# A five-layer graph network on one core: the first unit behind each batch norm rectified in two parts, and high pieces four units behind the rectifiers

## What is computed

```python
def _gin_conv(x, src, dst, edge_attr, w1, b1, bn_w, bn_b, w2, b2, ew, eb):
    edge_emb = edge_attr @ ew.T + eb
    n = x.shape[0]
    agg_x = jax.ops.segment_sum(x[src], dst, num_segments=n) + x
    agg_e = jax.ops.segment_sum(edge_emb, dst, num_segments=n) + eb
    h = jnp.concatenate([agg_x, agg_e], axis=1)
    h = h @ w1.T + b1                                  # to 256 features
    mean = jnp.mean(h, axis=0)
    var = jnp.mean((h - mean) ** 2, axis=0)
    h = (h - mean) * jax.lax.rsqrt(var + BN_EPS) * bn_w + bn_b
    h = jax.nn.relu(h)
    return h @ w2.T + b2                               # back to 128
...
h = jnp.maximum(_layernorm(x, axis=-1), 0.0)
for l in range(5):
    h = _gin_conv(h, ...)
    if l < 4:
        h = jax.nn.relu(h)
return x + h
```

## Time and profile before

| what | us |
|---|---|
| median of 3 runs | 654.82 (654.66 to 655.7) |
| the profiled execution, its own time | 658.63 |
| its span, first to last instruction | 656.8 |
| PE busy | 613.7 (93%) |
| VectorE busy | 331.2 (50%) |
| ScalarE busy | 261.0 (40%) |

### The profile page before, as it was taken

The page is one execution under the profiler, slowest core; times in us unless marked ns, Lnnn a source line. Parts: engine busy times, 40 slices in busy tenths (PEclk is TensorE's granted clock), DMA queues, the critical chain, the costliest instruction groups (busy, mean ns, idle before and its releaser), DMA issues.

```text
span 656.8 us, 12887 instructions
## 1 busy us (share of the span) xinstructions
PE 613.7 (93%) x5447; PEld 373.6 (57%) x5447; DVE 331.2 (50%) x663; ACT 261.0 (40%) x569; POOL 72.4 (11%) x90
## 2 busy tenths in 40 slices
PE   6788898978999989999999999999999999999996
PEld 6676787745555544844446644447544457444456
DVE  6799999979999928522113421125311216101034
ACT  0268977755677715601115411117211128012133
POOL 5550135510221100000000000000000000000000
PEclk9899999998999999999999999999999999999999
DMA  5981001000000000000000100000100000100033
GB/s 143 318 277 11 2 4 27 6 4 5 4 3 4 4 5 1 26 9 1 1 1 1 33 1 1 1 1 1 33 1 1 1 1 2 31 2 1 1 96 102
DMA packets 13320, 19.22 MB, mean 29 GB/s; under 512 B 2263, under 2 KB 7397, under 8 KB 13251
## 3 DMA queue, kind: packets, MB, share of 16 engines
q1 hardware_dynamic: 12099, 16.00, 8.1%
q0 software_dynamic: 1152, 2.20, 1.4%
HBM read 16.26 MB, written 1.60 MB: 27 GB/s over the span
## 4 chain that ended last, share of the span: by engine, by line
PE 59%; DVE 2%; ACT 1%; issue 0%; POOLq 0%; DVEq 0%
PE bank L1338 39%; PE bank L1402 9%; PE bank L1374 8%; PE bank L1368 2%; ACT h L1458 1%; DVE bn_stats L1562 1%; DVE h L1583 0%; DVE h L1584 0%; PE bank L1385 0%; PE bank L252 0%; DVE h L1603 0%; ACT bn_small L1471 0%; PE bank L1327 0%; DVE bn_small L1578 0%; DVE bn_small L1577 0%
## 5 line engine op out<-in xcount | busy, mean ns | idle before, releaser
L1338 PE MATMUL bank<-adj,h_pieces 128*128 128x504 bf16 (+1 forms) x1372 | 263.5, 351 | 0.0
L1338 PEld LDWEIGHTS bank<-adj,h_pieces 128*128 128x128 f16 x1372 | 123.0, 97 | 141.4 <-issue 10.2
L1562 DVE BATCH_NORM_STATS2 bn_stats<-bank 128x6 f32<-128x504 f32 (+1 forms) x70 | 42.8, 627 | 219.3 <-PE bank L1374 218.7
L971 ACT ACTIVATE adj<-bank 128x450 bf16<-128x450 f32 x175 | 95.3, 547 | 65.3 <-PE bank L829 60.0
L1449 ACT ACTIVATE aggT<-bank 128x504 f32<-128x504 f32 x24 | 14.2, 590 | 261.0 <-PE bank L1374 223.7
L444 DVE TENSOR_TENSOR h<-iota_lo,h 128x1536 bf16<-128x1536 bf16 (+2 forms) x95 | 87.5, 921 | 8.2 <-PE bank L829 7.1
L853 PE MATMUL bank<-h,adj 128*17 128x40 f32 (+11 forms) x1752 | 79.3, 206 | 11.2 <-DVE h L639 6.2
L829 PE MATMUL bank<-h 128*128 128x75 bf16 x1064 | 69.3, 201 | 17.5 <-DVE h L444 16.1
L453 PE MATMUL bank<-adj,h_pieces 128*128 128x450 bf16 x343 | 83.6, 356 | 1.6 <-issue 1.6
L829 PEld LDWEIGHTS bank<-h 128*128 128x128 bf16 x1064 | 54.9, 100 | 49.8 <-DVE h L444 30.0
L853 PEld LDWEIGHTS bank<-h,adj 128*17 128x17 f32 x1752 | 69.2, 104 | 18.1 <-DVE h L639 10.5
(11 more groups left out here) (151 smaller groups left out, 364.5 us busy)
## 6 DMA issues: line engine op xcount, KB each, us to landing
adj<-attr SPq DMA_DIRECT2D x1, 2524.5 KB
adj<-attr SPq DMA_DIRECT2D x1, 1963.5 KB
weights<-wpack SPq DMA_DIRECT2D x5, 323.0 KB
out<-h SPq DMA_DIRECT2D x6, 256.0 KB
adj<-attr SPq DMA_DIRECT2D x1, 1402.5 KB
adj<-attr SPq DMA_DIRECT2D x2, 561.0 KB
h<-mpack SPq DMA_DIRECT2D x5, 179.0 KB
adj<-order SPq DMA_DIRECT2D x2, 202.0 KB, 2.9
```

The source lines that it names most:

```text
L971: nc.scalar.activation(out_view(u), bank_view(n % CNT_BANKS), ACT.Copy).then_inc(s_ev, 1)
L1338: last = nc.tensor.matmul(agg_ps[b][:, 0:w], hp[:, k, s, :], adj[:, k, c * LW:c * LW + w], start=(k == 0 and s == 0), stop=stop and s == p ...
L1562: V.bn_stats(stats[:, h, ds(c * 6, 6)], w1_ps[b][h][:, 0:cols]).then_inc(st_last if last and h == 1 else st_done, 1)
```

## The change

The first unit is rectified in two parts, its first tile (128 columns) and its other three (384 columns), on ScalarE (half 0) and on VectorE (half 1). PE's unit 0 waits for the first part before tile 0, and for the second before tile 1. A semaphore is added for ScalarE's first part; VectorE's now counts two steps a layer. And high(u) stands behind the rectifiers of unit u+4 on ScalarE, where it stood behind those of unit u+2.

```diff
--- before.py
+++ after.py
@@ -1247,6 +1247,7 @@
             mv_done = sem("bn_moments_done")
             sd_done = sem("bn_deviation_done")
             relu0_done = sem("first_unit_second_half_done")
+            relu_tile = sem("first_tile_first_half_done")
             bn_c = sem("bn_chain")
             bn_ready = sem("bn_ready")
             relu_done = sem("relu_done")
@@ -1255,8 +1256,9 @@
             hi_done = sem("high_piece_done")
             o_done = sem("out_added")
             o_st = sem("out_stored")
-            BN_STEPS = 4
+            BN_STEPS = 5
             WSTEPS, M_STEPS = 16, 4
+            HI_LAG = 4
 
             def tiles_of(u):
                 return 1 if u == UNITS - 1 else 4
@@ -1389,14 +1391,19 @@
                     def project(l, u, final):
                         if u == 0 and not final:
                             pe.wait_ge(w2_scaled, l + 1)
-                        pe.wait_ge(relu_done, l * UNITS + u + 1)
                         if u == 0:
-                            pe.wait_ge(relu0_done, l + 1)
+                            pe.wait_ge(relu_tile, l + 1)
+                            pe.wait_ge(relu0_done, 2 * l + 1)
+                        else:
+                            pe.wait_ge(relu_done, l * UNITS + u + 1)
                         if u >= 2:
 
                             pe.wait_ge(t_done, l * UNITS + u - 1)
                         r = rows_of(u)
                         for j in range(tiles_of(u)):
+                            if u == 0 and j == 1:
+                                pe.wait_ge(relu_done, l * UNITS + 1)
+                                pe.wait_ge(relu0_done, 2 * l + 2)
                             for h in range(2):
                                 a = u * UW + j * P
                                 last = nc.tensor.matmul(w2_ps[u % 2][0:r, j * P:(j + 1) * P], h1[:, h, a:a + r],
@@ -1461,21 +1468,28 @@
 
                     def relu(l, u):
 
-                        for h in range(1 if u == 0 else 2):
-                            v = h1[:, h, u * UW:min((u + 1) * UW, N_NODES)]
-                            last = nc.scalar.activation(v, v, ACT.Relu, bias=shift[:, h:h + 1], scale=scale[:, h:h + 1])
+                        def part(h, a, b):
+                            v = h1[:, h, a:b]
+                            return nc.scalar.activation(v, v, ACT.Relu, bias=shift[:, h:h + 1], scale=scale[:, h:h + 1])
+                        if u == 0:
+                            part(0, 0, P).then_inc(relu_tile, 1)
+                            last = part(0, P, UW)
+                        else:
+                            for h in range(2):
+                                last = part(h, u * UW, min((u + 1) * UW, N_NODES))
                         last.then_inc(relu_done, 1)
 
                     def normalise(l, final):
                         act.wait_ge(mv_done, l + 1)
                         nc.scalar.activation(sd[:, :], mv[:, :, 1], ACT.Sqrt, bias=cst[:, EPSC:EPSC + 1]).then_inc(sd_done, 1)
                         act.wait_ge(bn_ready, l + 1)
-                        for u in range(UNITS + 2):
+                        for u in range(UNITS + HI_LAG):
                             if u < UNITS:
                                 relu(l, u)
-                            if u >= 2 and not final:
-                                act.wait_ge(t_done, l * UNITS + u - 1)
-                                nc.scalar.activation(hp_view(u - 2, 0), unit_view(0, u - 2), ACT.Relu).then_inc(hi_done, 1)
+                            if u >= HI_LAG and not final:
+                                act.wait_ge(t_done, l * UNITS + u - HI_LAG + 1)
+                                nc.scalar.activation(hp_view(u - HI_LAG, 0), unit_view(0, u - HI_LAG), ACT.Relu
+                                                     ).then_inc(hi_done, 1)
 
                     def layer(l, final):
                         act.wait_ge(l_wp, (l + 1) * 16)
@@ -1577,11 +1591,12 @@
                         steps.then(V.tensor_tensor(ms, mean_b, scale, ALU.mult))
                         V.tensor_tensor(shift, wp[:, BNB:BNB + 2], ms, ALU.subtract).then_inc(bn_ready, 1)
 
-                        v = h1[:, 1, 0:UW]
                         dve.wait_ge(h1_ev, (l + 1) * CHUNKS)
                         dve.wait_ge(bn_ready, l + 1)
-                        steps.then(V.tensor_scalar(v, v, scale[:, 1:2], shift[:, 1:2], ALU.mult, ALU.add))
-                        V.tensor_scalar(v, v, 0.0, None, ALU.max).then_inc(relu0_done, 1)
+                        for a, b in ((0, P), (P, UW)):
+                            v = h1[:, 1, a:b]
+                            steps.then(V.tensor_scalar(v, v, scale[:, 1:2], shift[:, 1:2], ALU.mult, ALU.add))
+                            V.tensor_scalar(v, v, 0.0, None, ALU.max).then_inc(relu0_done, 1)
                         assert steps.n == BN_STEPS
 
                     def add_bias(l, u):
```

## The result

The changed kernel takes 657.56 us in the median of 22 runs, the one before 655.25 in 22 runs beside them. The ratio is 1.0027, 95% interval 1.0018 to 1.0035, so 1.8 us more (1.2 to 2.3). The two means, 657.40 and 655.63, differ by 1.8 as well, the two medians by 2.3. The forecast was +1.9. One execution of the kernel with the split alone, further down, took 1038.12 us at a mean granted clock of 0.557; it is left out of that kernel's ratio.

What follows compares the result with a forecast made beforehand. TensorE was taken as the bound, busy 613.7 of 656.8 us, with the head on its path. Four layers at +0.52 and the last at -0.19 gave +1.9 us on the 654.82 median: 656.8, range 655.2 to 658.0.

Steps and rivals of the forecast that it cites:

- The size and the place of the loss: Projection of the first four layers: TensorE waits at units 4 and 5, last unit starts 0.52 us later a layer.
- The step on the head: Unit 0's split rectifiers: first tile 0.51 us earlier, 0.31 given back, unit 1 0.19 to 0.20 us a layer earlier.
- the wait at unit 4: Projection: bias(2), queued behind low(0) on VectorE, comes late, so TensorE waits 0.56 us before unit 4.
- Low(0) waits: Sign in the changed profile: VectorE's low pieces wait for the high piece, about 1 us at the first.
- the second wait, in front of unit 5: Projection: after high(1) the same steps make TensorE wait another 0.14 us; sign given as 0.1 to 0.2.
- The last layer: No high pieces there, so only the head counts: -0.19 us, the residual's load just in time for unit 2.
- B: Rival: the wait at unit 4 does not bite, faster, -1.0 us (653.9) or -2.6 (652.3); chance 0.08.
- C: Rival: wait half as long, ScalarE's row shorter, loss 0.1 to 0.35 a layer; +0.8 us, 655.6; chance 0.22.
- D: Rival: split at its upper price or TensorE slow to restart behind each wait; +3.6 us, 658.4; chance 0.08.
- E: Rival: holes in the projection lower TensorE's granted clock to 1.2 GHz for two units; 14 us, 669; chance 0.02.

Runs made afterwards that it cites:

- the split alone: The changed kernel with `HI_LAG = 2` (two-part first unit, high pieces two units behind as before); 655.35 us, ratio 0.9995 to the kernel before.
- lag 5: The changed kernel with `HI_LAG = 5`, high pieces five units behind instead of four; 663.13 us against 655.41 for the kernel before, ratio 1.0117.
- the lag alone: The kernel before with high pieces four units behind, unit 0 in one part; 656.07 us against 655.46, ratio 1.0005.
- the change with the moved wait: The changed kernel, last layer's VectorE wait for the residual's load moved from first bias to first residual addition; 656.33 us, ratio 1.0014 to the kernel before.

## Why the prediction was right

**The size and the place of the loss: right.** The working set unit 4's start at R + 8.75 and unit 6's at R + 12.47. Measured are R + 8.73 and, by the bias of unit 5 less 0.27 us (the distance that the working had between the two), 12.44; unit 6's first record itself stands at R + 12.61, before at R + 12.12, the same 0.49. High(0) was put at R + 6.65 and came at 6.64, since ScalarE's spacing of 0.707 and the overlap of its parts held (128 columns took 493 ns for the 478 that I worked out, 384 took 693 for 692). The chain high(0), low(0), bias(2), unit 4 was shown by three doses: lag 4 without the split +0.21 a layer, with it +0.49, lag 5 +1.75; and by the run that takes the bias additions out from behind the low pieces and leaves the rest, -0.06.

**The step on the head: the price of VectorE's part was too low.** I took 256 ns for the multiply-add on 128 columns, from a line through 353 ns at 256 columns (L1514, one pointer) and 547 at 512 (L1583, two pointers). It took 348 ns, and 475 for 384, in the groups of lines by form of the changed kernel:

```profile
L1598 DVE TENSOR_SCALAR h<-h,bn_small 128x384 f32<-128x384 f32 x5 | 2.4, 475 | 0.0
...
L1598 DVE TENSOR_SCALAR h<-h,bn_small 128x128 f32<-128x128 f32 x5 | 1.7, 348 | 0.5
```

The two forms were not of one kind (one pointer and a multiply, against two pointers and a multiply-add). So unit 1 starts 0.06 us earlier, not 0.19. This cost the sum nothing in four layers, for the reason the prediction gave: the end of the projection hangs on ScalarE's row alone, and the head's gain is used up in front of the wait. But the wait at unit 4 was smaller too, where I had 0.56: without it unit 4 starts at R + 8.39, as the trace of the split alone has it, and it started at R + 8.73, 0.34 us later. Starting again cost another 0.07, since the first record behind a hole is 0.18 us ahead of the second where the spacing inside a group is 0.11; I had no term for that. The loss against before is nearly the same (0.49 for 0.52), since it is counted from before's start of unit 4. Two of my signs were off as well. Low(0) waits 1.57 us, and I wrote about 1 us where my own working gives 551.68 - 549.94 = 1.74. And the second wait, in front of unit 5, has 0.07 us where I had 0.14: unit 5's first record is 1.93 us behind unit 4's, 0.14 more than a unit's 1.787, and half of that is the new start.

**The last layer: mis-sized, and the sum came out in part by luck.** I had -0.19, with a margin of 0.02 us at unit 2 for the residual's load. The traced execution has +0.48. In eight traces (before, the change, and six of the runs above that keep the wait at bias(0)) bias(0) starts 7.90 to 8.65 us behind the issue of the load's second part, with the same instructions in front. The forecast took one early landing (7.90, the shortest of all) as the rule. The kernel before can wait for the load until R + 4.05 without loss (unit 2 asks at R + 4.88, and starts 0.83 behind bias(0) at the earliest); in its own trace the load was there at R + 3.76, in the other seven at R + 4.09 to R + 4.51. The run of the lag alone, with the last layer of the kernel before, has its bias of unit 5 at R + 12.77 behind a landing at R + 4.51; the change has 12.71 behind one at R + 4.45. So with a late landing the two are equal. Without any wait for the load the change has 12.16, beside the 12.23 of the early landing before, which is the 0.06 that the head gave. So the +0.48 comes from when the load happened to land in the two traced executions. The change's own part in this layer, estimated from these pairs, is 0 to -0.07, and the step of the working that was mis-sized is the -0.19. With the four layers that makes 1.9 to 2.0, beside the measured 1.8 (1.2 to 2.3). My sum was the same, but as 2.08 - 0.19: the four layers (4 x 0.49 = 1.96) were 0.12 too dear and the last one 0.12 to 0.19 too cheap. That the two cancel is luck.

**The rivals.** B (no wait, faster) is out: the wait is there in every lag of four or five with VectorE's order kept. C (half the wait) is out by the trace, 0.49 against its 0.1 to 0.35, though the lower end of the interval of the times would allow its upper edge, and the times of the change with the moved wait (+0.9) lie in C's range. D is out: ScalarE's split cost the 0.28 that the rows gave (high(0) at R + 6.64 for 6.36), and a new start of TensorE 0.07. E is out by the granted clock, which stayed at 1.00, the upper of its two levels, in the windows around the new holes. Each row has the window, its length, busy us (instructions) of PE, PEld, DVE, ACT and POOL, the granted clock, and DMA share and GB/s:

```profile
541.40:545.20 3.80, 3.65 (x20) 2.00 (x19) 2.47 (x11) 2.91 (x8) 0.00 (x0) 1.00 0.02 4
...
551.00:554.00 3.00, 2.83 (x24) 2.60 (x24) 2.36 (x5) 2.81 (x7) 0.00 (x0) 1.00 0.00 0
```

The short idles that the Trainium skill describes (TensorE: Matmul & The Clock Gate, A second HAM failure mode: psum-queue depth-cycling) did not lower it here. A rule of the Trainium skill that speaks against small tiles (VectorE: DVE Perf Modes, The TRN2 errata: a fixed extra latency per instruction, so tile 512 elements or more) agrees with the 348 ns for a quarter of the columns of a 547 ns instruction; yet the split into halves, 412 ns for 256 columns, paid all the same, since what counted was when the first part ended.

## What to carry to other kernels

When a piece of work that nobody seems to wait for is moved back on its engine, list what stands behind its consumer on the consumer's engine: here high(0) was in nobody's way, low(0) waited for it, and bias(2), queued behind low(0), freed TensorE's bank. Choose a split so that the second part ends just before the first part's work runs out: a quarter and three gave 0.06 us a layer, two halves 0.27, with the same number of instructions. Where a view's releaser is one of two semaphores that came at about the same time, move one of them and look again.

## What the runs showed of the hardware

- A TensorScalar with two pointers took 348, 412, 475 and 547 ns for 128, 256, 384 and 512 fp32 columns, so some 280 ns plus 0.51 per column at the small end. The one with a single pointer took 353 for 256, 59 less. It also has one operation (multiply) for their two (multiply and add), and other tensors, so which of these the 59 ns belong to is not shown. With an immediate and one operation (maximum) it was 228, 295, 361 and 428.
- Two adjacent instructions without a wait between them overlap: the multiply-add of the second part starts 0.09 us before the first part's maximum ends (543.69 against 543.55 + 0.23).
- The first fp32 matmul record behind a hole in the projection starts 0.18 us before the second, where the spacing is 0.11 otherwise (before at 545.60 and 545.79, after at 551.82 and 552.00): 0.07 us for each new start.
- The residual's load of 1.6 MB was there 7.90 to 8.65 us after its second part was issued, with nothing in the kernels to tell the executions apart. The scatter lies in the row of that issue on SyncE's queue, which takes 2.91 to 3.63 us in the eight traces (2.91 before, 3.58 after); from its end to bias(0) it is 5.0 to 5.1 us in all of them.
